# Twelve turns of maxima ahead of the main loop in place of fourteen, in a transformer layer's attention on one core

## The reference, cut to what matters

```python
q, k, v = proj(wq, bq), proj(wk, bk), proj(wv, bv)      # [B, 16, 1024, 8]
scores = jnp.einsum('bhqd,bhkd->bhqk', q, k) / math.sqrt(H)
attn = jax.nn.softmax(scores, axis=-1)                  # over 1024 keys
out = jnp.einsum('bhqk,bhkd->bhqd', attn, v)
x = layernorm(x + out_projection(out))
```

## Time and profile before

| | us |
|---|---|
| median of three runs | 442.44 |
| span of the profiled execution | 441.5 |
| TensorE matmul busy | 427.8 (97%) |
| VectorE busy | 386.5 (88%) |
| ScalarE busy | 367.7 (83%) |
| GpSimd busy | 90.3 (20%) |

### The profile page before, as it was taken

One profiled execution on the slowest core, in us unless ns is written; L12 is line 12 of the kernel. 1 busy time (PEld: TensorE's weight loads), 2 busy tenths in 40 slices (PEclk: granted clock), 3 DMA queues, 4 the chain that ended last, 5 costly groups with the idle time before them and its releaser, 6 DMA issues.

```text
span 441.5 us, 9824 instructions
## 1 busy us (share of the span) xinstructions
PE 427.8 (97%) x3496; PEld 227.0 (51%) x3498; DVE 386.5 (88%) x719; ACT 367.7 (83%) x694; POOL 90.3 (20%) x142
## 2 busy tenths in 40 slices
PE   8999999999999999999999999999899899999995
PEld 4543544444444444444444443544333488877884
DVE  6799999999999999999999999999884577657636
ACT  4487989998998999989899899999899886678762
POOL 9730000100000010000001002373311263046103
PEclk9999999999999999999999999999999999999999
DMA  6567741111130110113011001021021000000101
GB/s 165 176 196 129 270 147 33 44 28 28 48 122 25 45 31 28 27 48 122 25 46 33 26 27 49 14 43 47 15 39 50 13 8 1 1 2 2 48 1 48
DMA packets 17117, 24.88 MB, mean 56 GB/s; under 512 B 5169, under 2 KB 9009, under 8 KB 16689
## 3 DMA queue, kind: packets, MB, share of 16 engines
q1 hardware_dynamic: 16464, 23.68, 19.3%
q10 hardware_dynamic: 608, 0.59, 0.5%
HBM read 15.08 MB, written 7.60 MB: 51 GB/s over the span
## 4 chain that ended last, share of the span: by engine, by line
PE 76%; DVE 10%; ACT 5%; SPq 3%; DMA 2%; issue 2%; POOL 0%; POOLq 0%; DVEq 0%; ACTq 0%
PE ps L1369 24%; PE ps L1291 20%; PE ps L1479 16%; DVE negmax L977 9%; PE ps L1353 8%; ACT arena L664 2%; DMA parts_q<-arena 2%; PE ps L1223 2%; PE ps L1234 1%; PE ps L1423 1%; PE ps L1319 1%; PE ps L1263 1%; SPq L463 1%; SPq L435 1%; ACT v_pad L722 1%
## 5 line engine op out<-in xcount | busy, mean ns | idle before, releaser
L977 DVE TENSOR_REDUCE negmax<-ps 128x1 f32<-128x512 f32 x458 | 275.8, 701 | 1.8 <-PE ps L1291 1.5
L664 ACT ACTIVATE arena<-ps 128x512 f32<-128x512 f32 x360 | 190.0, 606 | 19.3 <-PE ps L1353 14.1
L1353 PE MATMUL ps<-qx,kx 64*128 64x512 f32 x512 | 171.3, 451 | 0.9 <-DMA qx<-mT 0.6
L1291 PE MATMUL ps<-kx,qx 61*128 61x512 f32 x468 | 160.2, 441 | 0.6 <-DMA qx<-parts_q 0.5
L1291 PEld LDWEIGHTS ps<-kx,qx 61*128 61x128 f32 x468 | 75.1, 184 | 88.6 <-DVE negmax L977 79.3
L1369 PE MATMUL ps<-arena,v_pad 128*32 128x256 f32 (+3 forms) x1328 | 104.8, 407 | 2.8 <-ACT arena L664 2.8
L664 ACT ACTIVATE hf<-ps 128x512 f32<-128x512 f32 x152 | 83.2, 604 | 9.4 <-PE ps L1353 8.4
L1353 PEld LDWEIGHTS ps<-qx,kx 64*128 64x128 f32 x512 | 78.9, 184 | 18.6 <-ACT arena L664 11.8
L1479 PE MATMUL ps<-hid,w_high 128*128 128x512 f32 (+1 forms) x296 | 68.3, 388 | 0.8 <-issue 0.4
L1479 PEld LDWEIGHTS ps<-hid,w_high 128*128 128x128 f32 x296 | 54.2, 188 | 12.3 <-issue 0.8
L1369 PEld LDWEIGHTS ps<-arena,v_pad 128*32 128x32 f32 x1328 | 28.5, 108 | 37.1 <-issue 30.7
(11 more groups left out here) (107 smaller groups left out, 317.2 us busy)
## 6 DMA issues: line engine op xcount, KB each, us to landing
qx<-parts_q SPq DMA_DIRECT2D x60, 64.0 KB, 2.1
late_sb<-in_late SPq DMA_DIRECT2D x3, 1280.0 KB, 5.5
kx<-parts_k SPq DMA_DIRECT2D x56, 64.0 KB, 2.2
parts_q<-prt SPq DMA_DIRECT2D x3, 512.0 KB, 6.4
parts_q<-arena SPq DMA_DIRECT2D x3, 512.0 KB, 8.3
xT_sb<-in_xT SPq DMA_DIRECT2D x4, 256.0 KB, 4.2
xT_sb<-arena SPq DMA_DIRECT2D x28, 32.0 KB
prt<-den SPq DMA_DIRECT2D x7, 128.0 KB
```

Source lines behind the costliest of these rows:

```text
L664: nc.scalar.activation(probs(n // HG)[:, heads(n), :], ps[:, PLAN["score", n][0], :], ACT.Exp, scale=SCALE).then_inc(exp_done, 1)
L977: nc.vector.tensor_reduce(negmax[:, t // TURNS % 2, m % 2, h * QT + q:h * QT + q + 1], ps[:, MAX_BANK + m % 4, :], AX.X, ALU.max, negate=T ...
L1291: nc.tensor.matmul(ps[:, half_bank(m), :], qx[at, slot, qc, h, q * P:(q + 1) * P], kx[at, slot, h, part * C:(part + 1) * C], start=True, s ...
L1353: nc.tensor.matmul(ps[:, bank, :], kx[at, slot, h % PAIR, kt * P:(kt + 1) * P], qx[at, slot, qc, h % PAIR, :], start=True, stop=True)\
```

## The change

`LEAD` becomes 12. What follows from it: `AHEAD` 56, `WHOLE` 25 (folded turns 5 to 24 in place of 5 to 26), `RUNS` 152, `TAIL` 115. Unit 0's maxima are turned after the pair that starts at t = 19 and copied after `copy_over(20)`. Their two row DMAs are issued one by SyncE's queue and one by ScalarE's, the latter between `copy_max(0)` and `copy_over(21)`, after a wait for the copy. `half_bank` and `probs` are adapted so that banks and buffers stay in step.

```diff
-LEAD = 14
+LEAD = 12
...
-TURN_AFTER, COPY_AFTER = 5, 6
+TURN_AFTER, COPY_AFTER = 3, 4
...
 def half_bank(m):
-    return MAX_BANK + (m + 2 * (FOLD // 2 + 1) if m < 2 * FOLD else m) % 4
+    return MAX_BANK + (m + 2 * (FOLD // 2) if m < 2 * FOLD else m) % 4
...
             if k >= TAIL:
-                return probs_2[:, (k - TAIL) % 2]
+                return probs_2[:, (k - TAIL + TAIL % 3) % 2]
             return hf if k % 3 == 2 else probs_2[:, k % 3]
...
                 store_q(0, i, 1, NG, q_out[0])
-            load_max(0, 0)
+            sp.wait_ge(max_copied, 1)
+            spread_max(sp, 0, 0)
             sp.wait_ge(k_out[0], STORE_INC)
...
                 if t == TURNS + COPY_AFTER:
                     copy_max(0)
+                    act.wait_ge(max_copied, 1)
+                    spread_max(act, 1, 0)
```

## The result

| | before | after |
|---|---|---|
| median | 442.48 us (442.43 to 442.78, 4 runs) | 448.39 us (448.25 to 448.65, 4 runs) |
| ratio, 95% interval | | 1.0128 [1.0111, 1.0146] |
| span of the profiled execution | 441.5 us | 446.9 us |
| mean granted TensorE clock | 1.000 | 0.984 |

The account below looks back on a forecast made before the run. VectorE's half turns were taken to set the main loop's pace. Maxima's end +1.24 us (-1.17 + 2.41) plus +0.15 in the tail gave +1.4 on the 441.5 us span; with 0.9 us for the median, 443.8 us, range 442.5 to 444.8.

Parts of the forecast that it names:

- Work of VectorE: Main loop: two folded turns go, four half turns of 0.602 us come, net +1.18 us on VectorE.
- SyncE's queue: Start: unit 0's turn one pair earlier, loads from 33.73 instead of 35.03 us, unit 1's rows 1.30 us sooner.
- The second queue: Start: unit 0's second row DMA issued by ScalarE, worth at most one issue to SyncE, less given the store's landing.
- ScalarE's queue: Start: row DMA ahead of ScalarE's copies takes 0.85 us (bounds 0 and 0.92), VectorE idles 0.7 us.
- The two paths: Up to unit 1's first score: the later of SyncE's -1.30 us and VectorE's -1.17 us counts, so -1.17 us.
- path A: Route to unit 1's first score through SyncE's queue: -1.30 us; if it held, the maxima's end moves +1.11 us.
- disputed 0.85 us: ScalarE's row DMA issue at the start; its cost was said to be worth 0.13 us at the maxima's end.
- The tail: Behind the last maximum: the dropped group of four scores, 2.08 us at first sight, ran covered in a 3.2 us wait; counted none.
- The copy of unit 15's maxima: Tail: turn and copy now stand behind the output projection, the copy costing ScalarE +0.15 us.
- slower still: Rival, 7%: SyncE late with row DMAs, some of 14 units stall, 0.1 us each, +1.4 us, 445.2 us.
- The turn ahead does nothing: Rival, 4%: at the start unit 0's turn is held up, loads start as before, 445.0 us.
- Faster, by the tail: Rival, 12% together with hidden half turns: the end follows the number of tail steps, 2.08 us go, 441.7 us.

Follow-up runs that it names:

- 14-turn kernel with the later projection: Kernel before, with only the output projection's first two pieces together one step later; 442.77 us beside 443.25, ratio 0.9985.
- one queue: Changed kernel with both row DMAs of unit 0 on SyncE's queue again, nothing else; 446.05 us beside 442.99, ratio 1.0072.
- filled start: Changed kernel plus five unread matmuls in TensorE's two waits at the start behind ScalarE's DMA; 446.35 us beside 442.95, ratio 1.0077.
- filled tail: Changed kernel plus 22 unread matmuls ahead of the projection's wait for the first normalization; 446.73 us, ratio 1.0069.
- second queue alone: Kernel before, with only unit 0's row DMAs spread over SyncE's and ScalarE's queues; 446.45 us beside 443.25, ratio 1.006.
- projection two steps later: Twelve turns, unit 0's row DMAs both on SyncE, projection's first three pieces together two steps later; 442.46 us, ratio 0.9977 against the kernel before.
- twelve turns with the later projection: Changed kernel, unit 0's row DMAs both on SyncE, projection's first two pieces one step later; 442.16 us, ratio 0.999; again 442.94 us, 0.9997.

## Why the prediction was wrong

The side was right and the size was not: +5.9 us against +1.4. Point by point, by its own steps:

- *Work of VectorE*, +1.18 us: right. 462 half turns at 0.602 us.
- *SyncE's queue*: right at the loads (33.71 for 33.73 us). Unit 1's row DMAs started 1.69 us sooner and not 1.30. The last store of batch 1 was issued at 43.79 us, only 0.78 us sooner than before, but it had landed by 51.49 us: at most 7.7 us and not 8.34. The chain "is unchanged" only in its instructions. Rows that come still sooner are worth nothing where VectorE's path is the later one. Why the landing shrank is open; in the 14-turn kernel with the later projection the rows started at 52.20 us, so it changes between executions of the same code.
- *The second queue*, "worth at most one issue to SyncE": it was worth nothing that shows. With two DMAs ahead of the loads (34.38 us) as with one (33.71 us), unit 1's row DMAs start at 51.45 and 51.49 us. That agrees with the rule of the Trainium skill that the prediction cites, by which at most the time of the issue is saved.
- *ScalarE's queue*, 0.85 us: mis-sized, 1.35 us. The bound of 0.92 was the same DMA on SyncE, where it takes 0.93 us here too; the price on ScalarE lies outside the bounds that were taken from rows of other situations. Both queues issue at 32.56 us here, and whether it is less when ScalarE issues alone was not tested. VectorE's gap of 0.7 us became 1.24.
- *The two paths*, -1.17 us: path A was to hold if ScalarE's issue cost nothing, with +1.11 us to the last maximum. With that issue gone it is -0.11: unit 1's rows were early enough that path A didn't count. With the issue in and the clock held it is +0.83 for a forecast of +1.24; with the clock free, +2.30. That the +0.83 is within 0.4 us of the forecast is in part luck: the gaps of 0.29 and 0.50 us that the forecast takes off were those of one execution, and against the 290.83 us of the same code without them it is +1.95. The "disputed 0.85 us" was worth not 0.13 us but 0.9 at a held clock and 2.4 in all.
- *The tail*, "What is left behind the projection is the same in both": this is the step that failed, since it put the clock behind the longer wait at nothing, and the start has the same hole. The scores and products that no longer run in the 3.2 us cost nothing as work, and the projection did start 3.19 us behind the maximum. But they had kept TensorE at work. The prediction looked at each wait for what it delays and never for what TensorE does in it: idle went from 0.86 to 2.67 us, the clock fell to half from 319.9 to 326.7 us, and 2.0 us were lost. Filling the wait with unread matmuls gives these back.
- *The copy of unit 15's maxima*, 0.15 us: the tail is 0.49 us longer with the clock held. 0.16 of it is TensorE's turn of the maxima, which the prediction moves to the tight side but doesn't price.

So the excess of 5.9 - 1.4 = 4.5 us is, by profiles of one execution each: in the tail 2.0 of clock (by filling) and 0.3 for the turn and copy; up to the last maximum 2.30 - 1.24 = 1.1, which is 1.3 to 1.5 of clock (by filling) less the 0.4 that the rest of the term was too high; 0.6 of a later first folded turn, which is spread; and 0.5 that the profiles don't show.

Of the rivals, *slower still* gave 445.2 us by late rows. It was on the right side with the wrong cause: VectorE waited for TensorE's half-turn matmuls 1.4 us in two places, both ahead of unit 1's first score, and not at the units behind. *The turn ahead does nothing* gave 445.0 us, but the loads did start sooner. *Faster, by the tail* had a true core. The 2.08 us step is to be had in the tail, but only if the projection moves too: fixed to step 114, the projection turned the dropped step into idle time. Even so the longer stretch ahead of the last maximum takes 1.0 to 1.9 us back.

Whether the falls are certain or only likely is partly open. All four runs of the changed kernel have a mean clock of 0.984, but with one queue the five runs compared go from 0.988 to 0.996, at 444.73 to 448.50 us.

## What to carry to other kernels

When a change takes covered work off TensorE ahead of a wait, ask how long TensorE will then stand idle in one piece, and read the granted clock of the windows behind the waits that already exist; the work was free, and the 22 unread matmuls put in its place didn't make the wait longer. When a step is dropped, look for pieces tied to an absolute step number and move them along. A DMA issue moved to a computing engine is priced at that engine's next instruction, and it saves time on the queue that it left only if no landing stands in that queue's way.

## What the hardware showed

- The same DMA of unit 0's rows, issued at the same time from two queues, took 0.93 us on SyncE and 1.35 us on ScalarE, in each of the six kernels that had it. ScalarE's next instruction stood behind the whole of it.
- TensorE idle for 2.67 us in the tail: the granted clock fell to its lower level each time (changed kernel, one queue, filled start), within the wait in the first and the third (at 319.9 and 319.3 us) and some 1.5 us after its end in the second. Idle for 0.86 to 0.88 us at the same place: it never fell, in six kernels. At the start it fell after 0.98 and 0.40 us (changed kernel), after 1.00 us alone (filled tail) and after 1.34 us alone (second queue alone); after 0.47 us alone it did not. At unit 1 it fell after 1.43 us (projection two steps later) and stayed whole after 1.00 us (the second profile of twelve turns with the later projection). So the length of one wait alone doesn't tell.
- Of the changed kernel's two stretches at half clock, each of 6.8 us, the one at the start cost 1.3 to 1.5 us and the one in the tail 2.0. In the tail 3.4 us at half clock cost 1.1 us with one queue and 1.5 us with the filled start, against the 30.82 us of the filled tail.
